# Attention output projection in a decoder layer: eight parts per window in four groups of two instead of six groups

## The chip, the cores and the metric

The kernel runs on one core of one Trainium2 chip. The metric is device time in microseconds (us), 1985.09 us as the median of three runs (1984.59 to 1986.24). The execution that the profile shows took 1984.65 us, of which the span from the first to the last instruction is 1982.9 us. A difference of about 0.2% (4 us) is what such a measurement can tell from no change.

## The reference, cut to what matters

A decoder layer on 16 batches of 256 tokens with 512 features: sliding-window attention, a convolution stage, a dense mixing stage. The change is in the attention.

```
y = layernorm(x)                              # 16 x 256 x 512
q, k, v = split(y @ qkv_w.T + qkv_b)          # 32 query heads, 8 key/value heads of 64
q, k = rope(q), rope(k)
logits = q k^T / 8, masked (causal, window of 128)
e = exp(logits - max); w = e / (sum(e) + exp(sink - max))
o = w v                                       # 16 x 256 x 2048
x = x + o @ out_w.T + out_b                   # the output projection
```

## The kernel before, in words

**Two sweeps, 32 windows.** The heads are done in two halves. A first sweep runs over the 16 batches with the weights of the first half, a second sweep over the same batches with those of the second half, and adds the two projections. One batch in one sweep is a *window*, numbered 0 to 31 here. A body covers two windows (`p` 0 to 7, `j` 0 and 1), and a last body, the drain, finishes windows 30 and 31 with no new batch (its two stretches are windows 32 and 33 by `y.window(p)`).

**Eight slots to a window.** The order of all engines is written out by hand in slots, `sl = 2 * (p % 4) + j`, 0 to 7. In each slot TensorE (PE) does, in this order:

- the transposes of a pair of heads' probabilities (L567), which need the DVE's division (`pn_ready`) and, since they reuse one PSUM bank, the DVE's masking of the transposed pair of the slot before (`pt_masked`, L927)
- in slots 0, 1, 3, 5, 6, 7 a *unit*: 24 matmuls of 128x256 that project q, k or v (L542, L535). All units write the same PSUM bank `wP`. Their results are read by ScalarE (ACT, L668) and then by VectorE (DVE, `turned`, L881), which counts `m_ready`; the next unit, or the next transposes of x, waits for that count
- in slots 2 and 4 of the first sweep the transposes of the next x (L481), into the same bank `wP`
- in slots 0, 2, 4, 6 the scores of four heads (L557) into the banks `sP`, after `masked`: the DVE's `mask_min` (L899, L905) must have read the previous scores
- the product of probabilities and v (L581)
- in slots 2 and 4 of the second sweep the transposes of the new x (L492)
- the parts of the output projection that `PARTS_AT` gives to the slot (L604)

**The parts.** A batch's projection is eight parts, `t, k = divmod(s, 4)`: parts 0 to 3 accumulate the first 128 rows in bank `oP`, parts 4 to 7 the second 128 rows. Each part is six matmuls of 128x512. The DVE adds the residual after part 3 and after part 7 (`RESIDUAL_AT`, slots 3 and 7, L949), and the first part of the next 128 rows waits for that (`x1_ready`). Before, slots 1, 2, 3, 4, 5, 7 hold parts 1 / 2, 3 / 4 / 5, 6 / 7 / 0 of the next batch.

**The other engines in a slot.** The DVE does: residual if any, division, masking of the transposed pair, `turned` for the unit, `mask_min` for the scores, the low part of the head outputs (`o_low`, L936), and layernorm pieces. `mask_min` follows `turned`, except in the second sweep, where slots 1 and 3 have it *ahead* of `turned` (`early`). ACT does: evacuation of the transposed pair, the unit's bias (`bent`, L668), `o_high` (L697), the exponentials (L681, L684).

```
            elif n == 0:
                wait(pe, m_ready, (QM + 1) * v)
            else:
                pe.wait_ge(m_ready, (QM + 1) * v + n)
```

These four lines of `unit_free` are the wait of a unit for `turned` of the unit before it, in slot 0 for that of slot 7 in the previous window. The transposes of x wait likewise (L474 to L477).

Of the kernel before, what the change touches and what calls it, by code (L numbers as in the profile page):

```python
# [27 lines left out]
B, T, D = 16, 256, 512  # L28
# [3 lines left out]
NKV, QM = 8, 4  # L32
# [82 lines left out]
def attention_part(nc, ctx, space, conv, mix, x, wqkv, bqk, bv, wout, bout, sinks, rope, masks, ident, factors, ssm_pad,  # L115
# [113 lines left out]
    NM, HM = 2 * B // 2, B // 2  # L229
    NS = NU + NO // 2  # L230

    def wait(eng, s, value):

        if isinstance(value, int) and value <= 0:
            return
        eng.wait_ge(s, value)
# [61 lines left out]
        return n if n < V_UNIT else n - 1  # L298

    RESIDUAL_AT = {3: 0, 7: 1}  # L300
    PARTS_AT = {1: [1], 2: [2, 3], 3: [4], 4: [5, 6], 5: [7], 7: [0]}

    def residual_tile(y, p, j):

# [2 lines left out]
    def parts_of(y, p, j):  # L307

        sl = 2 * (p % 4) + j
        if y.first and p < 7 or y.drain and p == 7 and j == 1:  # L310
            return []
        return PARTS_AT.get(sl, [])

# [154 lines left out]
    def tensor(pe):  # L468
# [114 lines left out]
            last.then_inc(pv_done, 1)  # L583

        def out_projection(y, p, s):
            back = 1 if s == 0 else 2
            v = y.window(p) - back
            o = (p // 4 - back) % 2
            t, k = divmod(s, 4)
            if t == 0:  # L590
                pe.wait_ge(ot_lo, 8 * v + 2 * k + 2)
            if y.first:
                pe.wait_ge(m_ready, QM + 1)
            if y.number in (0, 1):
                pe.wait_ge(lo_done, NU + k + 1)
            if y.number in (HM, HM + 1):
                if 2 * y.number + p // 4 - back == B and t == 0:
                    pe.wait_ge(lo_done, NS + NU + k + 1)
            if k == 0:
                wait(pe, x1_ready, 2 * v + t)  # L600
            steps = [(oTh, woh), (oTl, woh), (oTh, wol)]
            for c in (2 * k, 2 * k + 1):
                for n, (a, w) in enumerate(steps):
                    last = pe.matmul(oP[:], a[:, o, c, t * P:(t + 1) * P], w[:, c, :],  # L604
                                     start=(c == 0 and n == 0), stop=(c == NO - 1 and n == 2))
            last.then_inc(out_done, 1)
# [6 lines left out]
        def body(y):  # L613
            for p in range(8):
                for j in range(2):
                    if y.here(p, 3):
                        p_transposes(y, p, j)
                    n = unit_of(p, j)
                    if n is not None and not y.drain:
                        unit(y, p, n)  # L620
                    if x_next(y, p, j):
                        x_transposes(y.window(p) + 1, p % 4 - 1)
                    if j == 0 and y.here(p, 2):
                        scores(y, p)
                    u, jj = (p - 4, 1) if j == 0 else (p - 3, 0)
                    if y.here(u, 0):
                        pv(y, u, jj)
                    if x1_here(y, p, j) is not None:
                        x1_transposes(y.window(p) - 3, x1_here(y, p, j),
                                      (QM + 1) * 2 * B if y.drain else (QM + 1) * y.window(p) + 1 + p % 4)  # L630
                    if y.drain and p == 3 and j == 1:
                        conv.first_products(pe)
                    for s in parts_of(y, p, j):
                        out_projection(y, p, s)
# [884 lines left out]
def decoder_layer(nc, x, ctxt, wqkv, bqk, bv, wout, bout, sinks, ssm_pad, dcoef, factors, bias, rope, masks, ident, out):  # L1519
# [3 lines left out]
    with ExitStack() as ctx:  # L1523
        def sem(name):
# [23 lines left out]
                         qr_ready, masked, pt_masked, ot_lo, out_done, x1_ready, x1t_evac, tap_out, one_added, res_ready, res_placed)  # L1548
        mix = mix_part(nc, ctx, space, conv, x1_dram, bias, out, x1_stored, out_done, qk_done, qr_ready, f_in, one_added, res_placed)
        attention = attention_part(nc, ctx, space, conv, mix, x, wqkv, bqk, bv, wout, bout, sinks, rope, masks, ident, factors,  # L1550
                                   ssm_pad, dcoef, x1_dram, q2_dram, pad_dram, x1_stored, x1t_stored, qk_done, v_done, m_ready,
                                   sin_ready, v_ready, qr_ready, masked, pt_masked, ot_lo, out_done, x1_ready, x1t_evac, f_in,
# [87 lines left out]
```

## Time and profile before

| | |
|---|---|
| median of three runs | 1985.09 us (1984.59 to 1986.24) |
| profiled execution | 1984.65 us, span 1982.9 us |
| PE busy | 97% of the span |
| DVE busy | 78% |
| ACT busy | 48% |
| POOL busy | 44% |
| attention (windows 0 to 31 and drain) | from the start to about 1541 us |

PE is busy through nearly the whole span, and the chain of work that ended last lies on it for 85%. Where PE is never idle, a matmul less is time less, and an idle moment more is time more. A matmul's row gives its start; since matmuls overlap, the distance from one start to the next tells what a piece costs, not the row's own duration.

### The profile page before, as it was taken

The numbers are of one execution on the slowest core, as the hardware profiler recorded it, in microseconds if no ns is written. First come the engines' busy times: TensorE is split into PE (matmuls) and PEld (weight loads), VectorE is DVE, ScalarE is ACT, GpSimd is POOL, SyncE is SP. The second block draws the span as 40 slices with busy tenths as digits, with TensorE's granted clock in tenths as the row PEclk, the third lists the DMA queues.
The fourth block names the chain that finished last, engine by engine and source line by source line (L and its number), as shares of the span: only waits on it lengthen the run. The fifth ranks groups of instructions, "written<-read, shape, count | busy, mean of one in ns | idle before, by whom it ended". The sixth has DMA issues, their size and how long they took to land.

```text
span 1982.9 us, 45446 instructions
## 1 busy us (share of the span) xinstructions
PE 1930.0 (97%) x15708; PEld 1610.9 (81%) x15708; DVE 1547.7 (78%) x4948; ACT 954.6 (48%) x3534; POOL 866.7 (44%) x1000
## 2 busy tenths in 40 slices
PE   6899999999999999999999999999999999999899
PEld 6688888888888888888888888888886788887687
DVE  6777777777777777777777777777777799999887
ACT  4554555555555555555555555555554233333333
POOL 4444334333433343333333333333332588887554
PEclk9999999999999999999999999999999999999999
DMA  6147211111112122121111111111105655554333
GB/s 216 44 121 148 69 54 55 64 54 55 55 55 73 47 97 76 55 80 71 55 55 54 55 55 54 55 56 64 55 33 200 169 118 118 115 113 100 109 141 121
DMA packets 75828, 167.59 MB, mean 85 GB/s; under 512 B 7120, under 2 KB 19536, under 8 KB 75472
## 3 DMA queue, kind: packets, MB, share of 16 engines
q1 hardware_dynamic: 67008, 147.84, 23.7%
q0 software_dynamic: 3840, 8.39, 2.3%
q10 hardware_dynamic: 4752, 8.46, 1.1%
q8 instruction: 127, 2.08, 0.4%
q14 instruction: 101, 0.83, 0.1%
HBM read 114.08 MB, written 50.58 MB: 83 GB/s over the span
## 4 chain that ended last, share of the span: by engine, by line
PE 85%; DVE 9%; issue 2%; ACT 2%; POOL 1%; DMA 1%; DVEq 0%; SPq 0%; ACTq 0%; POOLq 0%
PE banks L542 22%; PE banks L604 18%; PE banks L581 9%; PE banks L557 9%; PE banks L1246 7%; PE banks L567 6%; PE banks L535 5%; PE banks L1474 5%; PE banks L1244 3%; DVE terms L1280 1%; ACT pr L681 1%; DVE banks L1298 1%; DVE banks L1290 1%; PE banks L492 1%; DVE terms L1301 1%
## 5 line engine op out<-in xcount | busy, mean ns | idle before, releaser
L681 ACT ACTIVATE pr<-pr,mx 128x128 f32<-128x128 f32 x1024 | 399.1, 391 | 354.3 <-DVE mx L905 354.3
L763 POOL TENSOR_TENSOR m<-m,rope_sb 128x512 f32<-128x512 f32 x160 | 206.5, 1291 | 512.7 <-ACT m L668 512.7
L542 PE MATMUL banks<-xTh,wh 128*128 128x256 f32 x1280 | 375.8, 294 | 2.3 <-DVE xTl L865 1.4
L542 PE MATMUL banks<-xTl,wh 128*128 128x256 f32 x1280 | 362.5, 283 | 0.0
L542 PE MATMUL banks<-xTh,wl 128*128 128x256 f32 x1280 | 362.0, 283 | 0.0
L914 DVE TENSOR_TENSOR den<-ac,es 128x4 f32<-128x4 f32 x256 | 51.6, 202 | 253.4 <-ACT es L684 253.3
L542 PEld LDWEIGHTS banks<-xTh,wh 128*128 128x128 f32 x1280 | 245.6, 192 | 4.2 <-issue 1.8
L542 PEld LDWEIGHTS banks<-xTl,wh 128*128 128x128 f32 x1280 | 246.0, 192 | 0.0
L542 PEld LDWEIGHTS banks<-xTh,wl 128*128 128x128 f32 x1280 | 245.2, 192 | 0.0
L1246 PE MATMUL banks<-kv,tap 128*128 128x288 f32 x864 | 238.4, 408 | 2.1 <-DMA tap<-padded_taps 1.5
L905 DVE CUSTOM_DVE_ANT_0 pr<-banks,mask_sb 128x128 f32<-128x128 f32 x1024 | 234.8, 283 | 0.2
L780 POOL TENSOR_TENSOR sk<-mx,sink_sb 128x4 f32<-128x4 f32 x256 | 59.8, 233 | 383.4 <-DVE mx L905 383.3
L581 PE MATMUL banks<-pT,vv 128*64 128x256 f32 (+1 forms) x2048 | 223.1, 339 | 1.7 <-DVE oTl L936 1.7
L604 PE MATMUL banks<-woh,oTh 128*128 128x512 f32 x512 | 220.5, 431 | 0.4 <-DVE x L949 0.4
L668 ACT ACTIVATE m<-banks,bqk_sb 128x256 f32<-128x256 f32 x320 | 134.2, 470 | 163.7 <-PE banks L542 163.4
L557 PE MATMUL banks<-kT,qT 32*128 32x128 f32 (+1 forms) x4096 | 203.8, 335 | 3.2 <-DVE mx L905 2.4
L581 PEld LDWEIGHTS banks<-pT,vv 128*64 128x64 f32 x2048 | 124.7, 136 | 97.8 <-issue 43.2
L604 PE MATMUL banks<-woh,oTl 128*128 128x512 f32 x512 | 200.9, 392 | 0.0
L604 PE MATMUL banks<-wol,oTh 128*128 128x512 f32 x512 | 200.8, 392 | 0.0
L881 DVE SCALAR_TENSOR_TENSOR m<-banks,bqk_sb,rope_sb 128x256 f32<-128x256 f32 x320 | 139.8, 478 | 77.5 <-ACT m L668 72.3
L919 DVE TENSOR_TENSOR pr<-pr,rden 128x512 f32<-128x512 f32 x256 | 188.2, 735 | 8.8
L681 ACT ACTIVATION_READ_ACCUMULATOR pr<-pr,mx 128x1 f32 x1024 | 191.3, 187 | 0.0
(120 smaller groups left out, 4192.4 us busy)
## 6 DMA issues: line engine op xcount, KB each, us to landing
kk<-in_ctxt SPq DMA_DIRECT2D x64, 192.0 KB, 3.6
x_in<-in_x SPq DMA_DIRECT2D x16, 512.0 KB, 3.5
xt_split<-xTh SPq DMA_DIRECT2D x16, 512.0 KB, 2.7
xt_split<-xTl SPq DMA_DIRECT2D x16, 512.0 KB, 4.0
xb<-in_x SPq DMA_DIRECT2D x16, 512.0 KB, 4.2
factors<-in_factors POOLq DMA_DIRECT2D x8, 1024.0 KB, 8.6
x_part_rows<-x SPq DMA_DIRECT2D x16, 512.0 KB, 3.0
xTh<-xt_split SPq DMA_DIRECT2D x16, 512.0 KB, 4.8
```

The lines of the kernel that those rows point to most:

```text
L542: last = pe.matmul(bank[:, h * T:(h + 1) * T], w[:, n, c, h * P:(h + 1) * P], a[:, s, c, :], start=(c == 0 and i == 0), stop=(c == KD - 1 ...
L557: last = pe.matmul(sP[:, r, t * P:P + 2 * t * P], qT[rr, p % 2, h, t * P:(t + 1) * P], kT[rr, kslot, h, 0:(t + 1) * P], start=(h == 0), st ...
L567: last = pe.transpose(pP[:, (2 * a + t) * P:(2 * a + t + 1) * P], pr[:, (2 * p + 2 + j) % 4, a, t * P:(t + 1) * P], id_sb[:])
L581: last = pe.matmul(vP[a * HD:(a + 1) * HD, k * P:T], vv[:, (u // 4) % 2, k, g * HD:(g + 1) * HD], pT[:, s, a, 2 * k * P:2 * P + k * P], st ...
L604: last = pe.matmul(oP[:], a[:, o, c, t * P:(t + 1) * P], w[:, c, :], start=(c == 0 and n == 0), stop=(c == NO - 1 and n == 2))
L668: last = act.activation(m2[:, s, 1 - half], bank[:, half * T:(half + 1) * T], ACT.Identity, bias=bqk_sb[:, y.sweep, i, half:half + 1])
L681: act.activation(pr[:, s, a, cols], pr[:, s, a, cols], ACT.Exp, bias=mx[:, s, i:i + 1], scale=-1.0, accum_out=ac[:, s, i:i + 1])
L763: pool.tensor_tensor(m2[:, s], m2[:, s], rope_sb[:, 1 if i == 0 else 0, 1:3], ALU.mult).then_inc(sin_ready, 1)
L881: last = dve.scalar_tensor_tensor(m1[:, s, half], bank[:, half * T:(half + 1) * T], bias[:, half:half + 1], tab[:, 0], ALU.add, ALU.mult)
L905: last = dve.tensor_tensor_reduce(pr[:, s, a, t * P:(t + 1) * P], sP[:, 2 * j + a, 2 * t * P:(2 * t + 1) * P], mask_sb[:, t * P:(t + 1) * ...
L919: dve.tensor_tensor(quarters, quarters, rden[:, s].unsqueeze(2).broadcast_to([P, 2 * NT, P]), ALU.mult).then_inc(pn_ready, 1)
L1246: last = pe.matmul(y[:, s, c, 0:NY], tap[:, k, block], kv[:, s, c - d, :], start=(d == 0), stop=(d == c))
```

## The change

The table `PARTS_AT` changes. Slots 1, 2, 4, 5 now hold two parts each, slots 3 and 7 none. Part 0, which stood in slot 7 of the window before, comes in slot 1 with part 1. All eight parts of a batch are thus done in one window, and the bookkeeping of which batch and buffer a part belongs to becomes simpler. No instruction is added or removed, on any engine: 192 parts' groups become 128. Only PE's order changes; DVE, ACT, POOL and the DMA queue keep theirs.

```diff
     RESIDUAL_AT = {3: 0, 7: 1}
-    PARTS_AT = {1: [1], 2: [2, 3], 3: [4], 4: [5, 6], 5: [7], 7: [0]}
+    PARTS_AT = {1: [0, 1], 2: [2, 3], 4: [4, 5], 5: [6, 7]}
...
         sl = 2 * (p % 4) + j
-        if y.first and p < 7 or y.drain and p == 7 and j == 1:
+        if y.first:
             return []
         return PARTS_AT.get(sl, [])
...
         def out_projection(y, p, s):
-            back = 1 if s == 0 else 2
-            v = y.window(p) - back
-            o = (p // 4 - back) % 2
+            v = y.window(p) - 2
+            o = p // 4
             t, k = divmod(s, 4)
             if t == 0:
                 pe.wait_ge(ot_lo, 8 * v + 2 * k + 2)
-            if y.first:
-                pe.wait_ge(m_ready, QM + 1)
-            if y.number in (0, 1):
+            if y.number == 1:
                 pe.wait_ge(lo_done, NU + k + 1)
-            if y.number in (HM, HM + 1):
-                if 2 * y.number + p // 4 - back == B and t == 0:
+            if y.number == HM + 1:
+                if p < 4 and t == 0:
                     pe.wait_ge(lo_done, NS + NU + k + 1)
```

On PE, from slot 7 of one window into slot 0 of the next, the order before has the six matmuls of part 0 (L604) between the products with v (L581) and the next transposes and unit (L567, L542); `banks` are the PSUM banks, `woh` and `wol` the projection's weights, `oTh` and `oTl` the head outputs:

```order
L581 MATMUL banks<-pT,vv 64x256 x2
L581 MATMUL banks<-pT,vv 64x128 x2
L604 MATMUL banks<-woh,oTh 128x512
L604 MATMUL banks<-woh,oTl 128x512
L604 MATMUL banks<-wol,oTh 128x512
L604 MATMUL banks<-woh,oTh 128x512
L604 MATMUL banks<-woh,oTl 128x512
L604 MATMUL banks<-wol,oTh 128x512
L567 MATMUL banks<-id_sb,pr 128x128 x4
L542 MATMUL banks<-xTh,wh 128x256
```

The same place on PE in the changed kernel:

```order
L581 MATMUL banks<-pT,vv 64x256 x2
L581 MATMUL banks<-pT,vv 64x128 x2
L567 MATMUL banks<-id_sb,pr 128x128 x4
L542 MATMUL banks<-xTh,wh 128x256
L542 MATMUL banks<-xTl,wh 128x256
```

The part has moved to slot 1, so only four short transposes and the products with v now stand between the end of unit 7 and the start of the next unit.

On PE, from slot 3 into slot 4 in the first sweep, the order before (L481 transposes the next x into the units' bank, L557 are the scores of four heads):

```order
L581 MATMUL banks<-pT,vv 64x256 x2
L581 MATMUL banks<-pT,vv 64x128 x2
L604 MATMUL banks<-woh,oTh 128x512
L604 MATMUL banks<-woh,oTl 128x512
L604 MATMUL banks<-wol,oTh 128x512
L604 MATMUL banks<-woh,oTh 128x512
L604 MATMUL banks<-woh,oTl 128x512
L604 MATMUL banks<-wol,oTh 128x512
L567 MATMUL banks<-id_sb,pr 128x128 x4
L481 MATMUL banks<-id_sb,xn 128x128 x4
L557 MATMUL banks<-kT,qT 128x128 x8
```

The same place in the changed kernel:

```order
L581 MATMUL banks<-pT,vv 64x256 x2
L581 MATMUL banks<-pT,vv 64x128 x2
L567 MATMUL banks<-id_sb,pr 128x128 x4
L481 MATMUL banks<-id_sb,xn 128x128 x4
L557 MATMUL banks<-kT,qT 128x128 x8
```

Part 4 has moved into slot 4, behind the scores that here follow the transposes.

## Rows read from the trace of the kernel before

**Rows 1.** Page, the chain that ended last, shares of the span by engine.

```profile
PE 85%; DVE 9%; issue 2%; ACT 2%; POOL 1%; DMA 1%; DVEq 0%; SPq 0%; ACTq 0%; POOLq 0%
```

**Rows 2.** Waits on PE: engine, line, releaser: us in total, times, longest.

```profile
PE banks L567 <- DVE pT L927: 12.4, 14, 1.4
...
PE banks L604 <- DVE x L949: 0.4, 1, 0.4
```

**Rows 3.** Windows 1, 5, 24: busy PE, PEld, DVE, ACT, POOL; clock, DMA share, GB/s.

```profile
45.00:97.00 52.00, 42.52 (x418) 34.90 (x416) 38.81 (x156) 28.75 (x115) 22.61 (x26) 1.00 0.15 54
239.25:285.94 46.69, 46.69 (x425) 39.30 (x424) 36.18 (x136) 24.03 (x100) 17.62 (x22) 1.00 0.16 58
1124.04:1170.54 46.50, 46.50 (x425) 39.10 (x424) 34.79 (x134) 24.51 (x100) 15.13 (x20) 1.00 0.16 56
```

**Rows 4.** Timeline, slot 7 into slots 0, 1: start us, duration us, instruction.

```profile
236.95 0.87 PE L581 MATMUL banks<-pT,vv 128*64 128x256 f32 x8
...
238.07 0.88 DVE L881 SCALAR_TENSOR_TENSOR m<-banks,bqk_sb,rope_sb 128x256 f32<-128x256 f32 x2
...
239.25 0.60 PE L567 MATMUL banks<-id_sb,pr 128*128 128x128 f32 x4
...
239.60 0.36 PE L542 MATMUL banks<-xTh,wh 128*128 128x256 f32 x1
...
242.96 0.68 DVE L927 TENSOR_TENSOR pT<-banks,mask_sb 128x512 f32<-128x512 f32 x1
...
244.97 0.65 PE L567 MATMUL banks<-id_sb,pr 128*128 128x128 f32 x4
```

**Rows 5.** Timeline, window 1: a unit that waited for `turned`; idle before in brackets.

```profile
56.77 0.87 DVE L881 SCALAR_TENSOR_TENSOR m<-banks,bqk_sb,rope_sb 128x256 f32<-128x256 f32 x2 [0.19 <-ACT m L668]
...
57.70 0.39 PE L542 MATMUL banks<-xTh,wh 128*128 128x256 f32 x1 [0.35 <-DVE m L881]
```

**Rows 6.** Timeline, window 5 (first sweep), slot 3 into slot 4.

```profile
260.31 0.87 PE L581 MATMUL banks<-pT,vv 128*64 128x256 f32 x8
...
262.61 0.60 PE L567 MATMUL banks<-id_sb,pr 128*128 128x128 f32 x4
...
263.39 0.08 DVE L905 DVE_READ_ACCUMULATOR2_ANT mx<- 128x1 f32 x1
...
263.62 1.59 PE L557 MATMUL banks<-kT,qT 32*128 32x128 f32 x32
```

**Rows 7.** Timeline, window 2: scores that waited for the end of `mask_min`.

```profile
121.74 0.08 DVE L905 DVE_READ_ACCUMULATOR2_ANT mx<- 128x1 f32 x1
...
121.97 0.39 PE L557 MATMUL banks<-kT,qT 32*128 32x128 f32 x4 [0.27 <-DVE mx L905]
```

**Rows 8.** Timeline, window 24 (second sweep), slot 3 into slot 4.

```profile
1144.99 0.87 PE L581 MATMUL banks<-pT,vv 128*64 128x256 f32 x8
...
1145.55 0.08 DVE L905 DVE_READ_ACCUMULATOR2_ANT mx<- 128x1 f32 x1
...
1147.82 1.59 PE L557 MATMUL banks<-kT,qT 32*128 32x128 f32 x32
```

**Rows 9.** Timeline of PE, slot 4: a group of two parts, and what follows it.

```profile
265.94 0.50 PE L604 MATMUL banks<-woh,oTh 128*128 128x512 f32 x1
...
267.43 0.39 PE L604 MATMUL banks<-woh,oTh 128*128 128x512 f32 x1
...
268.80 0.60 PE L567 MATMUL banks<-id_sb,pr 128*128 128x128 f32 x4
```

**Rows 10.** Timeline of PE: transposes of slot 3 that waited, windows 2, 3, 15, 16.

```profile
114.73 0.63 PE L567 MATMUL banks<-id_sb,pr 128*128 128x128 f32 x4 [0.33 <-DVE pT L927]
...
163.01 0.63 PE L567 MATMUL banks<-id_sb,pr 128*128 128x128 f32 x4 [0.88 <-DVE pT L927]
...
724.82 0.63 PE L567 MATMUL banks<-id_sb,pr 128*128 128x128 f32 x4 [1.05 <-DVE pT L927]
...
771.24 0.63 PE L567 MATMUL banks<-id_sb,pr 128*128 128x128 f32 x4 [0.52 <-DVE pT L927]
```

## The prediction

> **What bounds the kernel now.** I read the chain first: it lies on PE for 85% [rows 1], so the order of PE's work is the time as long as PE does not wait. Then the waits on PE: the largest is 12.4 us over 14 times, and the wait for the projection's own bank, which the first part after a residual could suffer, is 0.4 us, once [rows 2]. So neither the DVE nor the bank `oP` holds PE up today: whatever the change relaxes there is worth at most those 0.4 us. Then the steady windows: window 5 of the first sweep takes 46.69 us with PE busy for all of it, window 24 of the second sweep 46.50 us likewise [rows 3]. Last I read, slot by slot, how far ahead of PE's need its releasers finish, since a full PE hides how near the next engine is.
>
> The nearness shows at two places. In the first sweep `mask_min` of slot 3 ends at 263.39 + 0.08 = 263.47, and the scores of slot 4 start at 263.62 [rows 6]. Where scores are known to have waited, they started at 121.97 after an end at 121.82 [rows 7]: 0.15 us, the same distance. The scores of slot 4 start at the first moment that the DVE allows, though the trace books no wait. And after unit 7 the DVE's `turned` starts 238.07 - 236.95 = 1.12 us after PE began the products with v, takes 0.88, so it ends at 2.00, while the next unit starts at 2.65 [rows 4].
>
> **The change part by part.** No instruction comes or goes, so all is in what the order exposes. I count from the start of the products with v (L581), which follow the unit directly.
>
> *A part's price.* In a group of two the first part takes 267.43 - 265.94 = 1.49 us, the second 268.80 - 267.43 = 1.37 [rows 9]. A part put behind another costs 1.37. A lone part removed gives 1.49, less 0.05 by which the transposes right behind the products are longer (0.65 against 0.60, rows 4): 1.44. If nothing waits, the change takes 2 x 1.37 on and 2 x 1.44 off each window: -0.14 us, about -4 us over 30 windows. That is all that fewer groups can give.
>
> *Slots 1 and 5, one part more each.* Windows 2 to 31: 30 x 2 x 1.37 = +82.2 us. PE is full there, so nothing hides them.
>
> *Slot 7, part 0 gone.* Without it PE would reach the unit of slot 0 at 2.65 - 1.44 = 1.21 us. But that unit writes the bank that ACT and the DVE still read for unit 7, and waits for `m_ready`. `turned` ends at 2.00 [rows 4]; the unit that waited for it started at 57.70 after an end at 57.64, 0.06 later [rows 5]. So it starts at 2.06: 0.59 saved instead of 1.44. Behind the waiting matmul stand the scores, the products and the next transposes, so the wait of 0.85 goes through in full. Over the 30 boundaries from window 1/2 to window 30/31: -17.7 us. Nothing can make `turned` earlier, since it follows unit 7 through ACT; bounds are 1.21 (no wait, another -26 us) and 2.65 (nothing saved, +18 us), and I take 2.06, which is read off rows. Does the next check still hold? The masking in slot 0 ends at 243.64 [rows 4], 6.69 after the products of slot 7; plus 0.15 it would release the transposes of slot 1 at 6.84. PE gets there at 2.06 + (244.97 - 239.60 = 5.37) = 7.43. It holds, by 0.6 us, and only because PE has just waited.
>
> *Slot 3, part 4 gone, first sweep.* PE would reach the scores of slot 4 at (263.62 - 260.31 = 3.31) - 1.44 = 1.87. `mask_min` there stands behind `turned`, which stands behind unit 3 and ACT, so `masked` stays at 3.16 and the scores at 3.31 [rows 6]. Saved: nothing. The transposes of x ahead of them wait too, for the same `turned`, at no further cost. Windows 2 to 14, 13 x 0. Bounds: -1.44 each (-19 us) and 0.
>
> *Slot 3, second sweep.* Here `mask_min` stands ahead of `turned` and ends at 1145.63, 0.64 after the products; the scores start at 2.83 [rows 8]. Without the part they start at 1.39, later than 0.64 + 0.15. All of it is saved: windows 15 to 31, 17 x -1.44 = -24.5 us.
>
> *Slots 2, 4, 6.* The parts 5, 6 and 4, 5 trade places in slot 4 at no price. The residual after part 3 is in slot 3, ahead of part 4 in slot 4; that after part 7 in slot 7, ahead of part 0 in slot 1.
>
> *Waits that go.* Four transposes of slot 3 waited 0.33 + 0.88 + 1.05 + 0.52 = 2.8 us for the DVE, which was late in slot 2 [rows 10]. Slot 1 is 1.37 longer now, and the DVE's lateness counts from unit 1. All four end: -2.8 us, between 0 and -3.
>
> *The drain.* No units, PE waits for the DVE there. A part taken from in front of a wait saves nothing and one put in front of a wait is free: each at one or two places, 1.4 us apiece. Between -3 and +4; I take +1.5 us.
>
> *Sum.* 82.2 - 17.7 - 24.5 - 2.8 + 1.5 = +38.7 us. On the profiled execution of 1984.65 us this gives 2023.4; the median of the runs is 0.4 us higher, so 2024 us. By window: the first sweep 46.69 + 2.74 - 0.59 = 48.8 us, the second 46.50 + 2.74 - 0.59 - 1.44 = 47.2 us.
>
> **Rivals.**
>
> *Only the group starts count (faster).* If the releasers had the room, the time falls by 4 us and by the 2.8 us of waits: about 1978 us. For it speaks that PE waits so little today [rows 2]. Against it, that this wait is small because a part stands at each of these places. Chance 0.04.
>
> *One of the two covers is not needed.* If the unit of slot 0 starts at 1.21, the time is 26 us less: 1998. If the scores of slot 4 in the first sweep can follow PE, it is 19 us less: 2005. Against both stand orders in the code, a bank that is read until `turned` ends. Chance 0.08 together.
>
> *The DVE falls behind for good.* The late unit of slot 0 pushes its own `turned` and `mask_min`; after slot 7 the DVE is busy without a gap until 6.69, and the `turned` of slot 0 would start only then, end at 7.57, and release unit 1 at 7.63, where PE wants it at 7.43 + 0.35 = 7.78. That is 0.15 us of room. If the DVE is 0.5 us later than the rows say, each window pays some 0.4 us more, and slot 0's transposes may wait beside: 30 x 0.4 = +12 us, 2036 us. The stretch around window 1 speaks for it: there PE has hardly any parts, and it was busy for only 42.5 of 52 us because the DVE and ACT need their time for each slot all the same [rows 3]. Against it, a new window holds PE for 47 to 49 us, which leaves them more time than now. Chance 0.15.
>
> *The clock.* Short idle moments, some 0.85 us each and 43 of them with those of slot 4, could bring PE's granted clock down. In window 1 PE waited for 9.5 of 52 us in pieces of about 1 us, and the granted clock was 1.00, which is 2.4 GHz [rows 3]. If it fell to 1.2 GHz for the 5.37 us behind each wait of slot 0, that would be 30 x 5.37 = +161 us, 2185 us. The Trainium skill has such a rule (TensorE: Matmul & The Clock Gate, section A second HAM failure mode: psum-queue depth-cycling): frequent small idles of TensorE between groups of matmuls, as it cycles through PSUM, make its clock go back and forth between the two levels. By that rule the change would be far worse than my sum; the trace's window 1 does not bear it out. Chance 0.01.
>
> **How the numbers follow.** The forecast, 2024 us, has 0.72; the rivals have 0.04, 0.08, 0.15 and 0.01. The forecast's own range is 2016 to 2030 (0.1 us per boundary on either side is 3 us, the drain and the vanished waits 3 each). For 8 in 10 the range reaches into the DVE's case and a little toward the unneeded cover: 2010 to 2035. A measurement tells 0.2% (4 us) from no change: faster than that is the first rival, 0.04; within it nearly nothing, 0.02, for a mixture of unneeded covers; slower 0.94.
>
> **What would show it.** In the profile after, PE's waits have two new rows: L542 for the DVE's L881, about 30 times 0.8 us, some 25 us, and the transposes of x (L481) and scores (L557) in 13 windows of the first sweep, together 1.4 us in each, 18 us. PE's busy time falls by some 4 us at most. Window 5 lasts 48.8 us, window 24 47.2 us. The transposes of slot 3 in windows 15 and 16 no longer wait. The prediction is wrong if the unit of slot 0 starts less than 1.9 us after the products of slot 7, if first-sweep windows are not longer than those of the second by some 1.6 us, or if a large new wait stands at slot 1.

## The result, and the profile after

| | before | after |
|---|---|---|
| median | 1986.12 us (1984.59 to 1986.29, 5 runs) | 2026.9 us (2026.29 to 2028.46, 5 runs) |
| ratio | 1 | 1.0209, 95% interval 1.0197 to 1.0221 |
| profiled execution | 1984.65 us, span 1982.9 us | 2026.72 us, span 2024.9 us |
| window 5, window 24 | 46.69 us, 46.50 us | 49.00 us, 47.30 us |

The change makes the kernel 41 us slower. The forecast was 2024 us. The chain of work that ended last, from the page of the kernel after, in shares of the span, answers to [rows 1]:

```profile
PE 78%; DVE 14%; issue 4%; ACT 2%; POOL 1%; DMA 0%; DVEq 0%; SPq 0%; POOLq 0%; ACTq 0%
```

PE lost 7 points of the chain, and the DVE gained 5. The waits on PE of the kernel after (engine, line, releaser: us in total, times, longest) answer to [rows 2]; lines behind L600 stand 3 lower than before:

```profile
PE banks L567 <- DVE pT L924: 15.3, 25, 2.3
PE banks L542 <- DVE m L878: 14.1, 32, 0.7
PE banks L557 <- DVE mx L902: 10.8, 17, 1.8
...
PE banks L481 <- issue: 7.4, 12, 0.6
```

Both foretold rows are there: the unit (L542) waits for `turned` 32 times, and the scores (L557) wait 17 times, the transposes of x (L481) 12 times, against 13 windows foreseen; together those two are 18.2 us, where 18 were foreseen (2.4 us of L557 stood there before). The view puts the waits of L481 down to "issue", that is, to nothing it can see. They start 0.10 us after the end of `turned` (in window 5 at 268.39, after 267.42 + 0.88 = 268.30), so they wait for it all the same. Windows 5 and 24 of the kernel after (us, then busy us of PE, PEld, DVE, ACT, POOL; clock, DMA share, GB/s) answer to [rows 3]:

```profile
243.32:292.32 49.00, 47.00 (x424) 39.26 (x425) 36.18 (x135) 24.17 (x101) 17.75 (x22) 1.00 0.15 55
1156.90:1204.20 47.30, 46.65 (x425) 39.12 (x425) 34.73 (x132) 24.42 (x101) 15.13 (x19) 1.00 0.16 57
```

PE's busy time is what it was, within 0.3 us, and the window is longer by what it waits. The granted clock is 1.00 (2.4 GHz) in both. PE's page row is 1934.5 us busy, 96% of the span, against 1930.0 and 97% before.

**The boundary of two windows.** The timeline of PE from slot 7 into slot 0 of window 24, kernel after (start us, duration us, instruction, idle before), answers to [rows 4]:

```profile
1155.99 0.87 PE L581 MATMUL banks<-pT,vv 128*64 128x256 f32 x8
1156.90 0.63 PE L567 MATMUL banks<-id_sb,pr 128*128 128x128 f32 x4
1158.13 0.36 PE L542 MATMUL banks<-xTh,wh 128*128 128x256 f32 x1 [0.61 <-DVE m L878]
```

The DVE's row of the same moment:

```profile
1157.11 0.88 DVE L878 SCALAR_TENSOR_TENSOR m<-banks,bqk_sb,rope_sb 128x256 f32<-128x256 f32 x2 [0.36 <-ACT m L665]
```

`turned` starts 1.12 us after the products with v and takes 0.88, as before; the unit follows at 2.14 us, where it stood at 2.65. So a part of 1.44 us went and 0.51 was saved.

**Slot 3 into slot 4, first sweep.** PE in window 5 of the kernel after, answering to [rows 6]:

```profile
266.30 0.87 PE L581 MATMUL banks<-pT,vv 128*64 128x256 f32 x8
267.10 0.66 PE L567 MATMUL banks<-id_sb,pr 128*128 128x128 f32 x4
268.39 0.63 PE L481 MATMUL banks<-id_sb,xn 128*128 128x128 f32 x4 [0.64 <-issue]
269.61 1.59 PE L557 MATMUL banks<-kT,qT 32*128 32x128 f32 x32 [0.59 <-DVE mx L902]
```

The scores start 269.61 - 266.30 = 3.31 us after the products: to the hundredth where they stood with a part in between [rows 6]. The whole 1.44 us of it became waiting.

**A booked wait is less than the time lost.** At the boundary of window 24 the unit starts 1.23 us after the transposes instead of 0.35: 0.88 lost, 0.61 booked, since the transposes' modelled end covers the rest. In the first sweep part of the delay is booked to the transposes (L567) too. The row of 14.1 us therefore stands for some 26 us (an estimate, 30 x 0.88, with part of it in the row of L567). The distance between starts is the measure, and the booked wait only says who was waited for.

**Where the 42 us of span came from**, by starts of windows in the two traces; "foreseen" is the prediction's working sorted by the same borders:

| stretch | foreseen | measured |
|---|---|---|
| up to window 1 | 0 | +1.2 |
| window 1 | -1.4 | -1.3 |
| windows 2 to 14 (first sweep) | +26.7 | +25.5 |
| windows 15 to 17 | +0.6 | +3.1 |
| windows 18 to 31 (second sweep) | +9.9 | +10.7 |
| window 32 to the last part (drain) | +2.9 | +2.8 |
| after the attention | 0 | 0 |
| sum | +38.7 | +42.0 |

The 1.2 us at the start say nothing of the change: window 1 began anywhere from 49.6 to 51.0 us in the twelve kernels traced here, and at 50.6 in one whose windows 0 to 17 are those of the kernel before.

**The drain, and the clock.** The scores at the start of the drain follow the products of slot 7 at 3.31 us in both kernels, 1497.10 - 1493.79 before and 1537.70 - 1534.39 after, so part 0 was a cover there too and taking it out saved nothing. That is half of the +2.8; the other half is the second part in slot 5, where PE is full. The scores, before and then after:

```profile
1497.10 1.59 PE L557 MATMUL banks<-kT,qT 32*128 32x128 f32 x32 [0.41 <-DVE mx L905]
1537.70 2.77 PE L557 MATMUL banks<-kT,qT 32*128 32x128 f32 x32 [1.78 <-DVE mx L902]
```

The same 32 matmuls take 2.77 us instead of 1.59, because the granted clock was 0.50 (1.2 GHz) just then. The whole drain of the kernel before, and two stretches of the kernel after:

```profile
1496.09:1541.30 45.21, 40.37 (x271) 30.51 (x269) 31.26 (x101) 18.83 (x70) 9.33 (x13) 1.00 0.58 208
77.00:80.40 3.40, 3.40 (x36) 2.56 (x38) 1.86 (x6) 2.32 (x11) 0.09 (x1) 0.50 0.02 5
1537.90:1541.30 3.40, 3.40 (x36) 2.37 (x35) 1.87 (x5) 1.69 (x10) 0.29 (x2) 0.50 0.78 190
```

In the drain of this kernel the fall costs nothing, since PE would have waited for the DVE behind it: the products of slot 1 start 5.05 us behind the scores, against 5.02. In window 1, where PE also waits often, the clock fell in every kernel traced here but the one before. In the drain it fell in all but the one before and `before_mask_first`, and where no wait of PE stood behind the slow work it cost about 1.5 us. In windows 4 to 31 it fell in none of the twelve.

### The profile page after: what moved, and what is told of

Read it like the earlier page. It is cut to its first block, busy times and chain, and to the rows that moved or that the text cites. A ratio compares the mean times of both kernels' runs of the same rounds, so it can differ in the third digit from the quotient of the medians.

```text
span 2024.9 us, 45446 instructions
## 1 busy us (share of the span) xinstructions
PE 1934.5 (96%) x15708; PEld 1612.5 (80%) x15708; DVE 1544.9 (76%) x4948; ACT 953.0 (47%) x3534; POOL 864.4 (43%) x1000
## 4 chain that ended last, share of the span: by engine, by line
PE 78%; DVE 14%; issue 4%; ACT 2%; POOL 1%; DMA 0%; DVEq 0%; SPq 0%; POOLq 0%; ACTq 0%
PE banks L542 19%; PE banks L601 17%; PE banks L557 9%; PE banks L581 8%; PE banks L1243 6%; PE banks L567 5%; PE banks L535 4%; PE banks L1471 4%; PE banks L1241 2%; DVE m L878 2%; DVE terms L1277 2%; DVE pr L902 1%; DVE banks L1295 1%; DVE banks L1287 1%; DVE pT L924 1%
## 5 line engine op out<-in xcount | busy, mean ns | idle before, releaser
L542 PE MATMUL banks<-xTh,wh 128*128 128x256 f32 x1280 | 376.8, 294 | 15.6 <-DVE m L878 14.1
L542 PE MATMUL banks<-xTl,wh 128*128 128x256 f32 x1280 | 363.5, 284 | 0.0
L542 PE MATMUL banks<-xTh,wl 128*128 128x256 f32 x1280 | 363.1, 284 | 0.0
L542 PEld LDWEIGHTS banks<-xTh,wh 128*128 128x128 f32 x1280 | 246.6, 193 | 23.3 <-issue 20.9
L542 PEld LDWEIGHTS banks<-xTl,wh 128*128 128x128 f32 x1280 | 247.1, 193 | 0.0
L542 PEld LDWEIGHTS banks<-xTh,wl 128*128 128x128 f32 x1280 | 246.4, 193 | 0.0
L911 DVE TENSOR_TENSOR den<-ac,es 128x4 f32<-128x4 f32 x256 | 50.6, 198 | 245.7 <-ACT es L681 245.5
L581 PE MATMUL banks<-pT,vv 128*64 128x256 f32 (+1 forms) x2048 | 223.7, 339 | 1.3 <-DVE oTl L933 1.3
L557 PE MATMUL banks<-kT,qT 32*128 32x128 f32 (+1 forms) x4096 | 206.3, 338 | 11.8 <-DVE mx L902 10.8
L601 PE MATMUL banks<-woh,oTh 128*128 128x512 f32 x512 | 213.5, 417 | 0.4 <-DVE x L946 0.4
L581 PEld LDWEIGHTS banks<-pT,vv 128*64 128x64 f32 x2048 | 124.9, 136 | 98.6 <-issue 35.5
L694 ACT CAST oTh<-banks 128x256 fp32r<-128x256 f32 x256 | 95.5, 373 | 222.5 <-PE banks L581 221.4
```

Of the source, the lines that this page charges most:

```text
L542: last = pe.matmul(bank[:, h * T:(h + 1) * T], w[:, n, c, h * P:(h + 1) * P], a[:, s, c, :], start=(c == 0 and i == 0), stop=(c == KD - 1 ...
L557: last = pe.matmul(sP[:, r, t * P:P + 2 * t * P], qT[rr, p % 2, h, t * P:(t + 1) * P], kT[rr, kslot, h, 0:(t + 1) * P], start=(h == 0), st ...
L581: last = pe.matmul(vP[a * HD:(a + 1) * HD, k * P:T], vv[:, (u // 4) % 2, k, g * HD:(g + 1) * HD], pT[:, s, a, 2 * k * P:2 * P + k * P], st ...
```

## Experiments

Theory A: a lone part in slot 7 and one in slot 3 cover the hand-over of a bank from PE by way of ACT and the DVE back to PE, and without the part PE waits. Rival B: starting groups, the number of parts in a row, or a DVE that has fallen behind sets the time. Each ratio below is to the kernel before, with its 95% interval.

**Each half of the change alone.** First, part 0 stays in slot 7 (from the kernel before):

```diff
-    PARTS_AT = {1: [1], 2: [2, 3], 3: [4], 4: [5, 6], 5: [7], 7: [0]}
+    PARTS_AT = {1: [1], 2: [2, 3], 4: [4, 5], 5: [6, 7], 7: [0]}
```

> The changed kernel with part 0 back in slot 7 of the window before (the old bookkeeping), parts 4, 5 in slot 4 and 6, 7 in slot 5 as changed. Theory (two places lost their cover, each priced apart): slot 5 costs 30 x 1.37 = +41 us, slot 3 gives back 17 x 1.44 = -24.5 us in the second sweep and nothing in the first, slot 7 is as before. About 2002 us, first-sweep windows 48.05 us, second-sweep windows 46.4 us, no wait of a unit for turned. Rival (the whole loss sits at the unit of slot 0): about 1985 us. Rival (the DVE has fallen behind for good, so undoing one piece leaves most of the loss): above 2015 us.

Second, part 4 stays in slot 3 (from the kernel after):

```diff
-    PARTS_AT = {1: [0, 1], 2: [2, 3], 4: [4, 5], 5: [6, 7]}
+    PARTS_AT = {1: [0, 1], 2: [2, 3], 3: [4], 4: [5, 6], 5: [7]}
```

> The changed kernel with part 4 back in slot 3 (slots 4 and 5: parts 5, 6 and 7), part 0 in slot 1 as changed. Theory: slot 1 costs 30 x 1.37 = +41 us, slot 7 gives back only 30 x 0.5 = -15 us because the unit of slot 0 waits for turned of unit 7, the waits at slot 3 go (-3 us). About 2008 us, windows of both sweeps longer by 0.86 us than before (47.5 and 47.4 us). Rival (the loss sits at the scores of slot 4): about 1985 us. Rival (the DVE for good): above 2015 us.

The first took 2009.12 us (ratio 1.0122, 1.0105 to 1.0139), the second 2007.42 us (1.0113, 1.0098 to 1.0128). Their windows 5 and 24, the kernel with part 0 kept first:

```profile
244.08:292.15 48.07, 46.89 (x426) 39.28 (x425) 36.26 (x136) 24.03 (x100) 17.61 (x22) 1.00 0.16 55
1145.53:1191.97 46.44, 46.44 (x425) 39.08 (x424) 34.88 (x134) 24.20 (x100) 15.10 (x20) 1.00 0.16 57
```

and the one with part 4 kept:

```profile
238.77:286.37 47.60, 46.84 (x424) 39.27 (x425) 36.11 (x135) 24.15 (x101) 17.72 (x22) 1.00 0.16 57
1137.26:1184.60 47.34, 46.70 (x424) 39.12 (x425) 34.61 (x132) 24.72 (x101) 15.10 (x19) 1.00 0.16 57
```

Emptying slot 3 costs 1.38 us a window in the first sweep and gains 0.06 in the second; emptying slot 7 costs 0.80 and 0.85. Added up, that is 2.18 and 0.79 against the whole change's 2.18 and 0.79. (Window 5 is 0.12 to 0.14 above the others of its sweep where slot 7 is empty: 49.00 against 48.86 in the kernel after, 47.60 against 47.48 here.) In the steady windows the halves are independent, and each behaves as A says. Outside them they are not: windows 15 to 17 took 3.1 us and 1.5 us more than before and the drain 2.9 and 2.8, where the whole change has 3.1 and 2.8. So the two halves alone cost 24 and 22 us, and together 41. Part 0 kept is 7 us above what was expected although its windows are as expected: 3.1 us are in windows 15 to 17 and 2.9 in the drain. Some 1.5 of these 2.9 go with a fall of the granted clock to 0.50 at 1537.0, on work behind which PE did not wait: that slot takes 6.99 us instead of 5.43. The 2.8 of the other half has such a fall in it as well, at 1523.9.

**The wait of unit 0 taken away, the parts left as in the kernel after.** Unit 0 writes the projection's bank `oP`, which is free then; unit 1 may start on `wP` with `turned` of slot 7 done, and part 0 waits until unit 0 has been read:

```diff
+        if n == 0 and y.window(p) > 1:
+            return oP
...
-            elif n == 0:
+            elif n == 0 and v > 1:
+                wait(pe, x1_ready, 2 * (v - 2))
+            elif n == 0 or n == 1 and v > 1:
                 wait(pe, m_ready, (QM + 1) * v)
...
+            if s == 0 and not y.drain:
+                pe.wait_ge(m_ready, (QM + 1) * y.window(p) + 1)
```

> The changed kernel, but from window 2 on the unit of slot 0 writes bank oP, which is free between the residual of slot 7 and part 0 in slot 1, instead of wP. Nothing else moves. Theory: the wait of that unit for turned goes; what comes next is the release of slot 1's transposes by the DVE's masking (6.84 us after the products of slot 7 against 7.51 today) in the second sweep, and in the first the transposes of slot 0 that already wait about 0.5 us. 17 x 0.67 + 13 x 0.43 = 17 us less than the changed kernel: about 2010 us; second-sweep windows 46.65 us. Rival (PE was limited by the DVE's own speed there, the bank is no matter): 2027 us, no change from the changed kernel.

2010.85 us (1.0129, 1.0114 to 1.0144). PE in window 24:

```profile
1145.08 0.87 PE L585 MATMUL banks<-pT,vv 128*64 128x256 f32 x8
1145.98 0.63 PE L571 MATMUL banks<-id_sb,pr 128*128 128x128 f32 x4
1146.37 0.36 PE L546 MATMUL banks<-xTh,wh 128*128 128x256 f32 x1
...
1151.90 0.63 PE L571 MATMUL banks<-id_sb,pr 128*128 128x128 f32 x4
```

The unit now starts 1.29 us after the products. That is 0.85 sooner. Of it some 0.2 is lost again at the next transposes, 1151.90 - 1145.98 = 5.92 after the last ones instead of 5.7: they wait for the DVE's masking, which ended at 1151.08 + 0.68 = 1151.76. The second-sweep window fell to 46.60 us (46.65 expected), against 47.30. So the bank was the cause at slot 7. In the first sweep the unit starts at 1.56 to 1.69 us in most windows, because the transposes ahead of it wait for the DVE's masking. The Trainium skill (Perfetto Trace Analysis, section Optimizing Tensor Performance, Matmuls) states that independent groups of matmuls should rotate through PSUM banks so that one's evacuation overlaps the next group. These two kernels agree: 0.70 us a window in the second sweep for one bank more at one place. The kernel before had the same overlap from a part.

**The wait of the scores taken away in slot 3, first sweep.** `mask_min` goes ahead of `turned` in slot 3, and in slot 4 the scores ahead of the transposes of x; the second experiment does only the former:

```diff
-early = 2 * (p % 4) + j in (1, 3) and not fresh(y, p) and not y.drain
+early = 2 * (p % 4) + j in (1, 3) and (not fresh(y, p) or p % 4 == 1 and not y.first) and not y.drain
...
-if x_next(y, p, j):
+if x_next(y, p, j) and p % 4 == 1:
     x_transposes(y.window(p) + 1, p % 4 - 1)
 if j == 0 and y.here(p, 2):
     scores(y, p)
+if x_next(y, p, j) and p % 4 == 2:
+    x_transposes(y.window(p) + 1, p % 4 - 1)
```

> The changed kernel, but in slot 3 of the first sweep the DVE does mask_min ahead of turned (as the second sweep does), and in slot 4 PE does the scores ahead of the transposes of x. Theory: the first sweep's scores of slot 4 then start about 1.4 us after the products of slot 3 instead of 3.31, and 13 windows get 1.4 us shorter: 18 us less than the changed kernel, about 2009 us; first-sweep windows 47.45 us, second-sweep windows unchanged at 47.3. Rival (the DVE's total work, not its order, sets the first sweep): 2027 us.

> The changed kernel with mask_min ahead of turned in slot 3 of the first sweep, but the transposes of x still ahead of the scores in slot 4. Theory: the scores are then no longer held by masked, but by the transposes of x ahead of them, which wait for turned and start 2.1 us after the products of slot 3; so the scores start at about 2.65 instead of 3.31, and half of the 15 us comes back: 13 x 0.65 = 8 us, about 2018 us, first-sweep windows 48.2 us. Rival (only masked counts): 2011 us. Rival (only the transposes' wait counts): 2027 us.

Both together: 2011.6 us (1.0134, 1.0118 to 1.0149); the DVE's order alone: 2022.9 us (1.0190, 1.0176 to 1.0203). PE, slot 3 into slot 4 of window 5, both together:

```profile
265.37 0.87 PE L581 MATMUL banks<-pT,vv 128*64 128x256 f32 x8
266.17 0.66 PE L567 MATMUL banks<-id_sb,pr 128*128 128x128 f32 x4
266.76 1.59 PE L557 MATMUL banks<-kT,qT 32*128 32x128 f32 x32
268.28 0.66 PE L481 MATMUL banks<-id_sb,xn 128*128 128x128 f32 x4
```

No wait is left and the scores start at 1.39 us instead of 3.31. First-sweep windows are 47.52 us (47.45 expected), 1.34 shorter, second-sweep windows unchanged. With the DVE's order alone the transposes of x, still ahead, keep waiting for `turned`: the scores start 2.65 us after the products, the windows are 48.24 (48.2 expected). Its time is 5 us above the expectation. Some 2 are in windows 2 and 3, which did not get shorter, and 1.4 in the drain, where the granted clock was 0.50 from 1536.3 to 1539.7 on two parts for which PE did not wait. So two orders stood behind the wait of slot 4, and each had to be turned.

**All three at once, and the last without the change.** The kernel after with both remedies; then the second remedy on the kernel before:

> The changed kernel with both mends at once: unit of slot 0 in bank oP, and mask_min ahead of turned in slot 3 of the first sweep with the scores of slot 4 ahead of the transposes of x. Theory (two separate lost covers): the two gains, 16 and 15 us, add up: about 1996 us, first-sweep windows 47.0 us, second-sweep windows 46.6 us as with the bank alone. What is left over the kernel before is the transposes of slots 0 and 1 that wait for the DVE, windows 15 to 17 and the drain. Rival (the two share one shortage, the DVE's time): the second mend adds little, about 2008 us.

> The kernel before (six groups) with the same DVE order in slot 3 and scores ahead of the transposes in slot 4. Theory: part 4 in slot 3 covers the wait, and PE is full, so the mend is worth nothing there: 1985 us, within 0.1%. Rival (the scores of slot 4 were held back unseen in the kernel before too): 1980 us or less.

1997.64 us (1.0063, 1.0048 to 1.0079) and 1986.55 us (1.0007, 0.9998 to 1.0016). The remedies win back 29 of the 41 us, nearly the sum of 16 and 15 that they win alone. First-sweep windows last 46.9 to 47.3 us (47.0 expected), second-sweep windows 46.60. Of the missing 2 us, 1.4 are in the drain (4.1 instead of 2.8), where the clock fell to 0.50 from 1513.1 to 1516.5, on two parts that PE did not wait for. What stays over the kernel before is 13.7 us up to the last part: 5.3 in windows 1 to 14, 2.9 in windows 15 to 17, 1.2 in windows 18 to 31, 4.1 in the drain, 0.3 at the start. The order that mends the kernel after gives the kernel before nothing: where the part covers the wait, there is no wait to take away. Its steady first-sweep windows are 0.10 us longer, not shorter.

**More groups instead of fewer** tests whether starts matter. On the kernel before, in slots 2 and 4 the first part goes ahead of the products with v, the second stays behind, so six groups become eight:

```diff
+ahead = parts_of(y, p, j)[:1] if 2 * (p % 4) + j in (2, 4) else []
+for s in ahead:
+    out_projection(y, p, s)
 if y.here(u, 0):
     pv(y, u, jj)
...
-for s in parts_of(y, p, j):
+for s in parts_of(y, p, j)[len(ahead):]:
```

> The kernel before with the two parts of slots 2 and 4 apart, one ahead of the products with v and one behind them: eight groups a window instead of six, nothing else moved. It prices a group's start by itself. Theory: 0.12 us each as the first part of a group is longer than the second, 62 more groups: 5 to 7 us, 1991 us. Rival (a start is free, the row's length is hidden): 1985 us. Rival (the products come later and make the next wait longer): more than 1995 us.

1997.41 us (1.0063, 1.0051 to 1.0076), 6 us above the expectation. PE in slot 2 of window 24 with eight groups:

```profile
1145.19 1.59 PE L557 MATMUL banks<-kT,qT 32*128 32x128 f32 x32
1146.71 0.50 PE L604 MATMUL banks<-woh,oTh 128*128 128x512 f32 x1
...
1148.30 0.87 PE L581 MATMUL banks<-pT,vv 128*64 128x256 f32 x8
```

The part costs 1148.30 - 1146.71 = 1.59 us between scores and products, against 1.37 behind another part [rows 9] and 1.44 between products and transposes. So a start costs 0.22 us there and 0.07 at the places that this change touched. Its time fits the second rival of the expectation too (more than 1995 us, through longer waits). The traces rule that out: the steady second-sweep windows are 0.44 us longer, which is the two starts, no idle time is booked at these places, and the waits on L567 for the masking are 10.2 us against 12.4 before. B is right that starts have a price, and its size is too small to matter: two starts fewer in each of 30 windows, at 0.07, are the 4 us that the prediction allowed.

**Four groups of two at other places.** If only slots 3 and 7 needed cover, the pairs could stand in slots 1, 3, 5 and 7. All through, and then only from window 19 on (second sweep; window 18 changes over):

```diff
-    PARTS_AT = {1: [1], 2: [2, 3], 3: [4], 4: [5, 6], 5: [7], 7: [0]}
+    PARTS_AT = {1: [2, 3], 3: [4, 5], 5: [6, 7], 7: [0, 1]}
...
-            back = 1 if s == 0 else 2
+            back = 1 if sl == 7 else 2
```

> Four groups of two as in the change, but at the places that need cover: parts 0, 1 of the next batch in slot 7, parts 2, 3 in slot 1, 4, 5 in slot 3, 6, 7 in slot 5, in both sweeps; slots 2 and 4 have none. Theory (a group must stand between a unit and the next user of its bank): no unit waits for turned and no scores for masked. What is late next is slot 2 of the first sweep, now only 3.35 us long: the DVE's masking there ends 3.98 us after its start, so the transposes of slot 3 wait about 0.8 us in 13 windows, +10 us; two starts fewer a window give back 4 us or more. About 1992 us, second-sweep windows 46.3 us. Rival (the number of groups is what costs, a smaller number always gains): 1977 us.

> The kernel before up to window 17, and from window 18 on the four groups of two at slots 7, 1, 3, 5 (window 18 is the passage). In the second sweep the DVE's masking of slot 2 ends about 2.9 us after the slot's start, before PE needs it, so nothing new waits. Theory: two group starts fewer in some 14 windows at 0.07 to 0.2 us each, 2 to 5 us less than the kernel before: 1982 us. Rival (slots 2 and 4, short now, wait for the DVE in the second sweep too): 1990 us or more.

Both missed: 2024.44 us (1.0197, 1.0182 to 1.0213) and 2000.11 us (1.0078, 1.0065 to 1.0090). The waits on PE of the first have a second row here, that of L542 for ACT, that no other kernel had so far:

```profile
PE banks L567 <- DVE pT L927: 29.8, 29, 2.6
...
PE banks L542 <- ACT x_in L703: 8.6, 26, 0.3
```

PE at the end of slot 2, window 24:

```profile
1169.76 0.66 PE L492 MATMUL banks<-id_sb,xn 128*128 128x128 f32 x4
1170.25 0.60 PE L567 MATMUL banks<-id_sb,pr 128*128 128x128 f32 x4
1171.18 0.35 PE L542 MATMUL banks<-xTh,wh 128*128 128x256 f32 x1 [0.33 <-ACT x_in L703]
```

ACT in the same moment:

```profile
1170.45 0.58 ACT L703 COPY x_in<-banks 128x512 f32<-128x512 f32 x1 [0.21 <-PE banks L492]
```

The transposes of the new x in slots 2 and 4 (L492) write `wP` too, ACT copies it out until 1171.03, and the unit of the next slot follows 0.15 later, 0.58 us later than it would. Two parts stood in between, in the kernel before and in the change. Twice 0.58 is 1.16 a window; on 46.51 - 2 x 0.07 for two starts fewer that gives 47.5, and 47.57 was measured. In the first sweep the transposes of slot 3 waited 0.76 us (0.8 expected) and the steady window was 47.80, where 46.69 + 0.8 - 0.14 is 47.35. The same hand-over is behind this: the units of slots 3 and 5 start 0.25 us later each, 0.15 us after the DVE has read the transposed x out of `wP` (in window 5 the read ends at 265.20, the unit starts at 265.35). Windows 2 and 3 took 1.35 us each more than the steady ones did, and in each the granted clock was 0.50 for a stretch, from 118.4 and from 169.6. In window 2 PE had waited 1.96 us, until 117.23, before that. Since pairs at slots 1, 3, 5 and 7 lose as well, with the same number of starts as the change has, it is the place of a part that counts, not how many stand together.

No version tried here beats the kernel before. Its parts stand behind every place where `wP` changes hands in a hurry: slots 2 and 4 (by the last two runs), slot 3 of the first sweep, and slot 7. That slots 2 and 4 need theirs is read from the rows and the sum above; no run takes the bank away there.

## Why the prediction was right

*A full PE pays what is put on it.* Two parts more in slots 1 and 5 at 1.37 each: slot 1 is 7.11 us against 5.75, slot 5 7.05 against 5.68. That is right to a hundredth or so.

*Slot 7.* A new wait in every window, at 2.14 instead of 2.06 us. The step that was mis-sized is the distance from the end of `turned` to the unit: 1158.13 - (1157.11 + 0.88) = 0.14 us, where one pair of rows, from window 1, had given 0.06 [rows 5]. The trace before has a pair from the same boundary, window 0 into 1, that gives 50.67 - (49.65 + 0.88) = 0.14, and it was not used. Over 30 boundaries that is 2.4 us, seen as 0.79 a window instead of 0.71 in the second sweep. The other bank showed the cause.

*Slot 3.* Nothing saved in the first sweep, all in the second: 3.31 us in place, and 1.38 as forecast 1.39. Turning the orders showed the cause.

*The wait rows.* Some 25 us were expected in the row of L542 and 14.1 stand there. That was a wrong reading of the view, not of the time. PE's busy time was to fall by up to 4 us and rose by 4.5: the rows behind a wait are longer, such as 0.63 instead of 0.60 for the transposes, so busy time was no measure of what fewer starts give back.

*The waits that go.* They went at slot 3 of windows 2, 3, 15 and 16. Windows 2 and 3 even took 1.1 us less than foreseen. But windows 15 to 17 took 3.1 us more where 0.6 was foreseen. This is the step that failed. In window 15 of the kernel after, PE, slot 3 into slot 4:

```profile
754.88 0.87 PE L581 MATMUL banks<-pT,vv 128*64 128x256 f32 x8
756.29 0.63 PE L567 MATMUL banks<-id_sb,pr 128*128 128x128 f32 x4 [0.55 <-DVE pT L924]
757.46 1.59 PE L557 MATMUL banks<-kT,qT 32*128 32x128 f32 x32 [0.54 <-DVE mx L902]
```

The old wait of 1.05 us ahead of slot 3 is gone and two new ones stand behind it: the transposes of slot 4 start 1.41 us after the products instead of 0.80, the scores 2.58. In these windows the DVE has work that the steady ones lack, the low halves of the next sweep's weights (L868, 2.25 us at 745.35 and 1.21 us at 752.73 in window 15), and a removed part only brings PE to it sooner. The unit of slot 0 comes later too, 2.38 us after the products instead of 2.14, at the boundaries from 15/16 to 17/18. The prediction priced them like steady second-sweep windows. That it is this load on the DVE is read from the traces alone; all kernels with slot 3 emptied show it (+2.9 to +3.1 us), and with part 4 kept it is +1.5.

*The drain.* +2.9 us by these borders and +2.8 measured is luck in part. The term of +1.5 was a middle taken between -3 and +4, and the forecast had not looked at which slot of the drain is full. The same 2.8 also stands with either half of the change, with other causes in it.

*The sum.* 42.0 against 38.7 is closer than its parts: 2.5 us too little in windows 15 to 17 and 0.8 in the second sweep stand against 1.2 too much in the first, and 1.2 at the start are no part of the change.

*The rivals.* Fewer starts alone would have given 1978 us; the price of a start is real and small. Both covers were needed. The DVE did not fall behind for good: no wait for it stands at the unit of slot 1. The clock did not fall where this rival had it fall: a PE idle for 0.6 us at each of 30 boundaries was granted 1.00 in windows 5 and 24, and 0.995 as the mean of the span against 0.996 before. The Trainium skill's rule (TensorE: Matmul & The Clock Gate, section A second HAM failure mode: psum-queue depth-cycling), by which frequent small idles between groups make the clock go back and forth, did not apply to these. The argument for it was weak, though. The first line of [rows 3] starts 4.6 us ahead of window 1, which by itself (49.62 to 96.59) has 8.3 us of idle time in 47.0, and it was the only window 1 of the twelve without a fall: in the kernel after, the granted clock was 0.50 from 77.0 to 80.4 in the same window. A chance of 0.01 for the rival rested on one execution.

## What to carry to other kernels

Where an engine is full, a piece of work on it may still be a cover: ask of each piece that is moved what finishes on other engines while it runs, and compare the start of the next dependent instruction with the end of what would release it. Do this for every hand-over of the same buffer, those where nothing waits today above all, and for the first and last windows as well as the steady ones; the misses above came from looking only at the two places already known. Read the granted clock over the whole span of every kernel, not in chosen windows of one. When such a cover has to go, mend the hand-over (another bank, or the order of the reader) in the same step.

## What the runs showed of the hardware

- From the end of the DVE's or ACT's last read of a bank to the start of the matmul that waited for it, 0.14 to 0.15 us at the unit, the transposes of probabilities and the scores, and 0.10 at the transposes of x; one pair of rows had 0.06.
- A part costs 1.37 us behind another part, 1.44 alone between the products with v and the transposes, and 1.59 between scores and products, with no wait in any of them.
- Idle pieces of 0.3 to 0.8 us, once or several times in each window of 47 to 49 us, left the granted clock at 1.00 in windows 4 to 31 of all twelve kernels. Where PE waited more it fell to 0.50 now and then: at 77.0 and at 1537.9 in the kernel after. With the same waits in the drain it did not fall in the kernel before and fell in `eight_groups`, at 1515.6, so these runs don't tell what decides it.
